# Counted matmuls into an unused bank in the first front and the last back of a two-layer decoder

## What is computed

```python
x = _layernorm(x + _L0_attn_ref(x, ...))      # linear attention with decay, 16 heads
x = _layernorm(x + _L0_xattn_ref(x, ctx, ...))  # a 256x256 attention map on the context
x = _layernorm(x + _L0_ffn_ref(x, ...))       # gated FFN with 8 low-rank experts, top 2
x = _layernorm(x + _L1_attn_ref(x, ...))      # Mamba block: conv, selective scan, 16 states
x = _layernorm(x + _L1_xattn_ref(x, ctx, ctx))  # softmax attention, 32 heads of 8
x = _layernorm(x + _L1_ffn_ref(x, ...))       # 16 experts of 176, top 4, and a shared one of 704
```

## Time and profile before

| | |
|---|---|
| median of 3 runs | 1110.81 us (1109.4 to 1116.21) |
| the profiled execution | 1111.63 us, its span 1109.9 us |
| mean granted clock of TensorE | 0.918 |
| busy share of the span | PE 83%, DVE 64%, ACT 37%, POOL 36% |
| DMA, mean | 62 GB/s |

### The profile page before, as it was taken

The page is one execution under the profiler, slowest core; times in us unless marked ns, Lnnn a source line. Parts: engine busy times, 40 slices in busy tenths (PEclk is TensorE's granted clock), DMA queues, the critical chain, the costliest instruction groups (busy, mean ns, idle before and its releaser), DMA issues.

```text
span 1109.9 us, 16110 instructions
## 1 busy us (share of the span) xinstructions
PE 922.7 (83%) x4963; PEld 686.5 (62%) x4992; DVE 711.1 (64%) x1452; ACT 410.8 (37%) x902; POOL 396.7 (36%) x436
## 2 busy tenths in 40 slices
PE   5638445798999998699999998799989997685997
PEld 4426323574678786574678786664778785333886
DVE  4272569886446699695446799694456899743333
ACT  4101264333423754135323755126224753243221
POOL 2270348421015487130015587030024785000222
PEclk9868768799999999899999998899999998878999
DMA  5200300002003421202014330202012320200342
GB/s 192 102 1 0 140 0 0 1 2 102 2 16 106 162 82 34 83 2 102 1 31 144 109 93 22 84 1 102 1 58 82 103 87 0 82 1 1 105 151 81
DMA packets 21392, 68.46 MB, mean 62 GB/s; under 512 B 2668, under 2 KB 4460, under 8 KB 20148
## 3 DMA queue, kind: packets, MB, share of 16 engines
q1 hardware_dynamic: 21300, 67.32, 18.6%
HBM read 66.27 MB, written 1.05 MB: 61 GB/s over the span
## 4 chain that ended last, share of the span: by engine, by line
issue 33%; PE 31%; DVE 21%; POOL 7%; ACT 6%; DVEq 0%; POOLq 0%; DMA 0%; ACTq 0%; SPq 0%
PE B L781 19%; PE F L781 10%; DVE arena L1423 9%; POOL arena L489 2%; DVE nmx L1487 2%; POOL rs L457 2%; DVE q_t L1554 1%; ACT q_t L765 1%; ACT F L704 1%; POOL arena L478 1%; ACT arena L577 1%; POOL arena L490 1%; POOL arena L468 1%; PE B L1055 1%; ACT decay L573 1%
## 5 line engine op out<-in xcount | busy, mean ns | idle before, releaser
L781 PE MATMUL B<-k_t,mw 128*128 128x256 f32 x896 | 219.1, 389 | 0.0
L781 PEld LDWEIGHTS B<-k_t,mw 128*128 128x128 f32 x896 | 173.2, 196 | 26.0 <-issue 1.7
L558 POOL TENSOR_TENSOR k_t<-q_t 128x256 f32<-128x256 f32 x112 | 84.0, 751 | 240.7 <-DVE q_t L1559 232.4
L468 POOL TENSOR_TENSOR arena<-du,arena 128x1024 f32<-128x1024 f32 x64 | 150.3, 2357 | 32.3 <-ACT F L688 25.8
L704 ACT ACTIVATE F<-delta,a_neg 128x255 f32<-128x255 f32 x256 | 111.3, 467 | 125.1 <-DVE arena L1423 125.1
L1423 DVE TENSOR_TENSOR_SCAN arena<-F,arena 128x512 f32<-128x512 f32 x128 | 149.2, 1207 | 2.6 <-POOL arena L468 2.6
L781 PE MATMUL F<-arena,ident 128*128 128x256 f32 x384 | 112.6, 437 | 11.6 <-POOL arena L478 10.4
L781 PE MATMUL B<-mw,k_t 128*128 128x256 f32 x448 | 115.4, 382 | 0.6 <-POOL k_t L558 0.6
L1554 DVE SCALAR_TENSOR_TENSOR q_t<-q_t,B 128x256 f32<-128x256 f32 x112 | 47.1, 421 | 105.2 <-ACT q_t L765 104.4
L781 PEld LDWEIGHTS F<-arena,ident 128*128 128x128 f32 x384 | 79.3, 221 | 29.9 <-POOL arena L478 18.3
L781 PEld LDWEIGHTS B<-mw,k_t 128*128 128x128 f32 x448 | 81.9, 192 | 10.8 <-POOL k_t L558 1.0
(11 more groups left out here) (243 smaller groups left out, 1524.6 us busy)
## 6 DMA issues: line engine op xcount, KB each, us to landing
mw<-in_w_moe SPq DMA_DIRECT2D x112, 384.0 KB, 3.1
room<-in_w_f SPq DMA_DIRECT2D x4, 2672.0 KB, 9.6
room<-in_w_l SPq DMA_DIRECT2D x4, 1280.0 KB, 5.9
w_m<-in_w_m SPq DMA_DIRECT2D x1, 2112.0 KB
x_tok<-in_x_tok SPq DMA_DIRECT2D x4, 256.0 KB, 6.0
x_t<-in_x_t SPq DMA_DIRECT2D x4, 256.0 KB, 6.2
y<-x SPq DMA_DIRECT2D x4, 256.0 KB, 3.1
w_lb<-in_w_lb SPq DMA_DIRECT2D x1, 504.0 KB
```

What stands on the lines that cost most here:

```text
L468: g.tensor_tensor(state(n).rearrange("p d (s t) -> p d s t", s=2), du[:, 2 * dp:2 * dp + 2, :].unsqueeze(2).to_broadcast([P, 2, 2, S]), b_ ...
L558: g.tensor_tensor(hid1[:, m % 3, :], hraw[:, m % 2, :], crs[:, (m // 2) % 2, m % 2, :], ALU.mult)\
L781: return t_.matmul(dst, lhsT, rhs, start=start, stop=stop, skip_group_check=True)
```

## The change

Two tables give a number of calls for some steps. A helper `spin` issues that many float32 matmuls of the identity (as weights) with the first 256 columns of the constant tile `rows`. It starts and ends an accumulation each time, nobody reads the result, and no semaphore is bumped. In the front of batch 0 (`later(b)` is false for it alone) the calls go into bank B0, which no back uses yet. In the back of batch 3 (only there b is a plain integer) they go into F1, which no front uses any more. The calls stand ahead of the waits of their step. The loop, the other engines and the transfers stay as they were.

```diff
+IDLE_FIRST = {"xa": 8, "fa1": 28, "fa3": 18, "m2": 20, "d1": 6, "d3": 4, "s0": 9}
+IDLE_LAST = {"bq3": 11, "bg0a": 4, "br1": 9, "br3": 10}
...
+            def spin(bank, count):
+
+                for _ in range(count):
+                    mm(bank[:, 0:S], ident[:, :], rows[:, 0:S], True, True)
...
             def front(b, ph):
+                if not later(b):
+                    spin(K[0], IDLE_FIRST.get(ph, 0))
                 if ph == "qkv":
...
             def back(b, ph):
+                if isinstance(b, int):
+                    spin(F[1], IDLE_LAST.get(ph, 0))
                 if ph in ("bq1", "bq3"):
```

## The result

The changed kernel takes 1104.09 us in the median of 7 runs (1101.69 to 1106.92), the kernel before 1111.61 beside it: ratio 0.9915, 95% interval 0.989 to 0.9941. The forecast was 1097.0 with a range of 1091 to 1103, made from a kernel before of 1110.81 us; on that time the ratio gives 1101.4, inside the range, while the median itself, beside a slightly slower 1111.61, lies 1 us above it. The gain is 0.85% (0.6 to 1.1%), smaller than the forecast 1.2%. It is clear of zero, but within the 1% that was to count as no change.

A forecast was written before the change was run, and what follows sets the result against it. TensorE's clock falls during waits in the first front and last back, slowing the products behind. Gains of 9.3 (front) and 5.0 (back), 14.3 us together, give 1097.3 or 1096.5 by starting time; forecast 1097.0, range 1091 to 1103.

The forecast's parts named there:

- xa: First front: 8 calls hidden in a 3.88 us wait; products behind them gain 0 to 2.1 us, taken as 1.1.
- fa3: First front, ready x2 to zz's transposes: 18 calls, filler ends last; gain 2.0 us, 0 if five calls run low.
- FFN: First front, behind zz: transposes 0.4, z_t,w_lb 1.1, gate and up 1.7 us; 3.2 us gained.
- m2: First front: 20 calls hidden in a 9.69 us wait; transposes and first input projection instructions behind gain 2.2 us.
- d1: First front: 6 calls against a 2.98 us wait; products behind gain 0 to 1.6 us, taken as 0.8.
- bq3: Last back: 11 calls against a 5.84 us wait; the 32 transposes go from 3.57 to 1.95 us, gain 1.6.
- bg0a: Last back: four calls into a 2.01 us wait; up to 1.4 us late, first scores return up to 1.3; taken as 0.
- br1: Last back: 9 calls against a 4.44 us wait; transposes 0.4 and router product 0.9, gain 1.3 us.
- br3: Last back: 10 calls against a 5.39 us wait; transposes 0.1, gate and up 1.8, mask products 0.2, gain 2.1 us.
- Rival 2: Transposes in the five groups and bq3 take the same time at either clock; 3.7 us missing, 1101 us; chance 0.05.
- Rival 4: Given a chance of 0.03; the prediction describes no rival under this number.
- Rival 1: The clock comes up too late, or fillers stick out, as at fa1 (4.0 us late): 1102 us; chance 0.17.

The follow-up runs named there:

- front-only run: The changed kernel without the fillers of the last back (IDLE_LAST = {}), those of the first front kept; ratio 0.9966 to the kernel before.

## Why the prediction was right and where it was wrong

The mechanism was right in the stretches that were edited: fillers of 0.43 us hold the clock at 1.00, with one dip, and the products behind them run at the high pace. On the time that the forecast was made from, the result is 0.4% above it, in the 0.27 for "within 1%", because the loop took back 8 us. Term by term, from the intervals between the same rows in the two traces (those of before in the earlier trace rows):

| place | forecast | measured | from |
|---|---|---|---|
| start to xa's transposes | 0 | -0.4 | 49.61 to 49.99 |
| xa to xb's transposes | 1.1 | 2.25 | 20.37 to 18.12 |
| fa3, ahead of zz | 2.0 | 0.0 | 15.69 to 15.68 |
| FFN | 3.2 | 2.9 | 36.74 to 33.80 |
| m2 | 2.2 | 2.2 | 14.03 to 11.81 |
| d1 | 0.8 | 1.4 | 11.40 to 10.04 |
| bcp to the first mark | 0 | 0.0 | 73.98 to 73.97 |
| bq3 | 1.6 | 1.6 | first mark of the back to VectorE's maxima, 12.65 to 11.04 |
| bg0a | 0 | -0.4 | 66.13 to 64.95 at x5, less bq3 |
| br1 | 1.3 | 1.2 | 9.04 to 7.80 |
| br3 | 2.1 | 2.3 | the rest of the back |
| loop | 0, luck of 2 | -8.0 | 727.64 to 735.67 |

- **xa.** I took the middle, since no row told whether the clock stands through half-array products. It does: 1.08 and 1.13 us at 51.33 and 52.87. The full end, 2.1, was right. That the sum of the two stretches is near is in part luck: xa and d1 gave 1.7 us more than forecast, fa3 2.0 less.
- **fa3.** The forecast had TensorE reach the transposes of zz 13.7 us behind x2, "set by the filler", with a gain of "0 if the clock is low for five of the calls". Both came. The front-only run has the same program in its first front, and no dip of the clock:

```profile
68.39 0.63 PE L796 MATMUL F<-ident,xb 128*128 128x128 f32 x4 [1.82 <-DVE xb L1226]
69.70 1.30 PE L785 MATMUL F<-room,xt 128*128 128x152 f32 x8 [0.69 <-ACT xt L581]
70.84 3.62 PE L785 MATMUL F<-xt,room 128*128 128x256 f32 x16
74.29 7.93 PE L785 MATMUL B<-rows,ident 128*128 128x256 f32 x36
82.06 0.60 PE L982 MATMUL F<-ident,zz 128*72 128x128 f32 x4
```

  There x2 to zz takes 13.67 us, the filler ends last (no bracket), and VectorE had zz at 80.78. In the profiled execution of the changed kernel the clock was 0.50 from 69.5 to 72.9 us: the router product took 2.32 us instead of 1.30, the 16 instructions behind it 4.31 instead of 3.62, and the filler ended 15.5 us behind x2 (83.62). VectorE got its scores 0.7 us later (72.00 for 71.26, though x2 was 0.3 earlier), then sat out GpSimd's mask instructions at other places, and had zz at 83.74, so TensorE waited another 0.17. The step that failed is the high clock between x2 and zz, "half of 2.39" for the router product. The dip stands in six of the seven profiled executions with these calls at xa and fa1. What decides it is open: the wait ahead of it is 1.82 us with and without a dip. The filler's other part, behind zz, came.
- **FFN, m2, d1, and the back** came within 0.6 us each; xp's transposes, at 117.59, are behind the 114 to 116 named as a sign, by what fa3 did not give. At bg0a the four calls ran low and stuck out: 1.3 us from the maxima's cast to their transposes, of which the first scores gave back 0.9. That is inside the two ends given.
- **The loop** is the step that decided the result: "The loop in between is not edited. Where in it the clock dips can shift by luck, some 2 us to either side." Not edited was taken for not moved. The 372 instructions moved its head to 7 ahead of a block's end, and each of two returns pays 2.6 to 3.2 us: 5.8 of the 8.0 us are the gaps themselves. Of the other 2.2, 1.5 stand at the end of the third pass, where the clock was 0.50 from 943.3 to 946.8 us: `F<-arena,ident` at 942.98 takes 1.76 us and `F<-w_m,arena` behind it 4.72, where the kernel before had 1.13 and 3.85. That is the luck the forecast spoke of; loops without gaps took 724.4 to 734.4 us in the profiled executions here, so it is nearer 5 us to either side than 2. With the gaps taken away by twelve instructions the ratio is 0.987; on the 1110.81 us from which the forecast was made that is 1096.4, beside 1097.0.
- **The rivals.** Rival 2, the transposes' time, falls by 956.88 (1.95 for 3.57) and 49.99 (0.66). Rival 4 falls by the fillers' own rows. Rival 1's low clock appeared only at bg0a and in the dip at 69.5, behind the filler and not under it. The result came out near rivals 1 and 2 in number (1104 against 1102 and 1101) for a cause that was none of them. What I missed was a rival on code layout, for which the profile before had the rows: jumps of the loop with 3.78 us and more of "issue" or waits in front, and 16 KB packets in the instruction queue.

## What to carry to other kernels

An instruction that costs nothing where it stands still moves every loop head behind it: compare the first rows after each return in both traces, and if a group that was whole breaks there, shift the head by a few instructions before the change is judged (0.987 with twelve more, 0.9915 and 0.9924 without). Before a wait is filled with work, ask what the wait is made of: 5 of the 14 us at fa1 and all of the one at fa3 went when GpSimd wrote its mask behind zz, and taking them away gave as much (1.3%) as filling all the waits did with the loop's gaps removed (1.3%); the two together gave 2.7%. A filler earns what the products behind it save and nothing of the wait itself.

## What the runs showed of the hardware that was not expected

- A loop head 7 instructions ahead of the end of a 16 KB block costs 2.6 to 3.2 us at each jump back on TensorE (six jumps in three profiled executions of two kernels with fillers, and two in one without); with 51 or more left there was no gap. A packet of the instruction queue took 0.9 to 1.4 us of each gap.
- A float32 product of one column with 128x128 weights took 0.21 us at the low clock (8.53 us for 40), the pace of one of 256 columns at the high clock (7.93 for 36), and the granted clock was 0.50 from 152 to 169 us while TensorE was busy with them and little else. The weight loads were busy for 15.04 of 15.10 us there, which makes them the likely pace:

```profile
149.70:164.80 15.10, 15.10 (x84) 15.04 (x83) 9.28 (x8) 6.08 (x15) 10.65 (x6) 0.57 0.00 0
```

- A VectorE TENSOR_SCALAR or COPY that reads and writes SBUF alone, of 2 to 256 elements, lasted until about the end of the GpSimd memset or select beside it: up to 3.1 us instead of 0.2 to 0.4. In the front-only run a SCALAR_TENSOR_TENSOR of 16 elements with both operands in SBUF did so too (2.14 us, 0.18 with the mask moved). MAX8 (0.17) and MATCH_REPLACE8 (0.16) in SBUF, and instructions with an operand in PSUM (0.42), were not held.
